# A graph transformer layer with a mixture of experts: index loads first, the lane chain ahead of the last four tiles, and a final stage with 21 buffers

## The reference

```
xn = layernorm(x)
x1 = x + l2norm([xn, mean of xn[src] over dst] @ W) + bias + linear_attention(xn)
x2 = layernorm(x1)
# router: graph attention over the 131072 edges and one loop per node, 4 heads, 4 experts
e     = leaky_relu(a_src[src] + a_dst[dst])          # a = x2 @ (W_gat . att)
alpha = softmax of e over the edges of one dst
agg   = sum of h[src] * alpha over dst               # h = x2 @ W_gat
score = mean over heads of layernorm(agg + b)
gate  = softmax of the two best scores, 0 elsewhere
out = x1 + sum over the 4 experts of gate[e] * (gelu(x2 @ W1[e] + b1[e]) @ W2[e] + b2[e])
```

## Time and profile before

| | |
|---|---|
| Time, median of 3 runs | 5569.49 us (5564.70 to 5574.14) |
| The profiled execution | 5532.89 us, its span 5531.1 us |
| PE busy | 3498.8 us, 63% of the span |
| POOL busy | 2828.8 us, 51% |
| DVE busy | 2089.8 us, 38% |
| ACT busy | 793.1 us, 14% |
| HBM | 392.03 MB read, 146.74 MB written |

### The profile page before, as it was taken

The page is one execution under the profiler, slowest core; times in us unless marked ns, Lnnn a source line. Parts: engine busy times, 40 slices in busy tenths (PEclk is TensorE's granted clock), DMA queues, the critical chain, the costliest instruction groups (busy, mean ns, idle before and its releaser), DMA issues.

```text
span 5531.1 us, 46201 instructions
## 1 busy us (share of the span) xinstructions
PE 3498.8 (63%) x12938; PEld 2286.8 (41%) x12938; DVE 2089.8 (38%) x4906; ACT 793.1 (14%) x1914; POOL 2828.8 (51%) x2951
## 2 busy tenths in 40 slices
PE   0688888888577777777242766666666666669300
PEld 0455555555455545555121443434343434346200
DVE  5466665566466545444110111202021111103288
ACT  4111111111011111111010101111111111112000
POOL 2666666666666666666657044445445353530420
PEclk6799999899788889888575888787778878789755
DMA  7444444444355555555121011111111111111287
GB/s 241 127 116 114 114 114 114 111 115 113 109 137 147 149 143 157 167 150 147 23 57 19 32 49 33 47 35 44 38 43 46 36 46 36 46 31 63 85 258 258
DMA packets 381412, 540.56 MB, mean 98 GB/s; under 512 B 120314, under 2 KB 297818, under 8 KB 381143
## 3 DMA queue, kind: packets, MB, share of 16 engines
q0 software_dynamic: 119136, 234.44, 17.7%
q1 hardware_dynamic: 239503, 284.45, 15.8%
q10 hardware_dynamic: 22632, 20.15, 1.1%
HBM read 392.03 MB, written 146.74 MB: 97 GB/s over the span
## 4 chain that ended last, share of the span: by engine, by line
PE 24%; another core or an unknown queue 13%; issue 7%; DVE 3%; DVEq 2%; DMA 1%; ACT 0%; SPq 0%; ACTq 0%
PE PS L1668 14%; PE PS L1660 10%; DVE acc L1589 2%; DVEq L1588 1%; DMA out<-acc 1%; ACT hid L1629 0%; DMA x2g<-x_turned 0%; DVE rec L1418 0%; DVE y_sb L1603 0%; DVE sc L1553 0%; SPq L1287 0%; DVE rden L1528 0%; ACTq L1649 0%; DVE q L1523 0%
## 5 line engine op out<-in xcount | busy, mean ns | idle before, releaser
L773 POOL DMA_INDIRECT rows<-xn_rows,gsrc x1664 | 1606.2, 965 | 881.2 <-issue 455.9
L1339 POOL DMA_INDIRECT nb<-route_rows,idx x1024 | 999.6, 976 | 1082.8 <-DVE msg L1414 767.7
L1668 PE MATMUL PS<-arena,hid 128*125 128x256 f32 x3200 | 771.0, 400 | 555.6 <-ACT hid L1629 339.4
L1078 PE MATMUL PS<-rows,oh 128*128 128x257 f32 x3328 | 891.2, 421 | 281.5 <-issue 207.2
L1660 PE MATMUL PS<-x2g,arena 128*128 128x500 f32 x1600 | 754.6, 631 | 284.8 <-issue 148.3
L1668 PEld LDWEIGHTS PS<-arena,hid 128*125 128x125 f32 x3200 | 632.8, 199 | 710.7 <-issue 578.9
L1603 DVE TENSOR_TENSOR y_sb<-PS,b_b 125x512 f32<-125x512 f32 x200 | 128.7, 685 | 2004.6 <-PE PS L1668 1467.7
L1078 PEld LDWEIGHTS PS<-rows,oh 128*128 128x128 f32 x3328 | 684.9, 212 | 411.3 <-issue 242.9
L1660 PEld LDWEIGHTS PS<-x2g,arena 128*128 128x128 f32 x1600 | 319.6, 203 | 698.7 <-issue 535.7
L1629 ACT ACTIVATE hid<-PS,b_sb 128x500 f32<-128x500 f32 x400 | 270.3, 677 | 1547.5 <-PE PS L1660 758.5
L1150 PE MATMUL PS<-own_w,p_t 128*125 128x512 f32 x400 | 237.2, 678 | 124.4 <-issue 68.8
(11 more groups left out here) (303 smaller groups left out, 3093.0 us busy)
## 6 DMA issues: line engine op xcount, KB each, us to landing
y_rows<-y_sb SPq DMA_DIRECT2D x100, 512.0 KB
arena<-y_rows SPq DMA_DIRECT2D x100, 512.0 KB
rows<-xn_rows,gsrc POOLq DMA_INDIRECT x1664
nb<-route_rows,idx POOLq DMA_INDIRECT x1024
sum_rows<-kept SPq DMA_DIRECT2D x104, 128.5 KB
x_rows<-x SPq DMA_DIRECT2D x100, 128.0 KB
hid<-x_rows SPq DMA_DIRECT2D x100, 128.0 KB
m_in<-sum_rows SPq DMA_DIRECT2D x100, 125.5 KB
```

The source lines that it names most:

```text
L773: pool.indirect_dma_start(out=rows[w][h][:, q, 0:D], out_offset=None, in_=xn_rows, in_offset=bass.IndirectOffsetOnAxis(ap=gsrc[:, s * HU + ...
L1078: last = mm(SUM[:, 0:D + 1], oh[w][h][:, q, :], rows[w][h][:, q, :], start=h == 0 and q == 0, stop=h == 1 and q == HU - 1)
L1339: pool.indirect_dma_start(out=nb[b % NBUF][:, c, :], out_offset=None, in_=route_rows, in_offset=bass.IndirectOffsetOnAxis(ap=idx[:, b * W ...
L1668: last = mm(Y[j % 2][e // 2][0:NP, (e % 2) * D:(e % 2 + 1) * D], hid[:, 4 * e + k, j * NP:(j + 1) * NP], w2_sb[:, e, k, :], start=k == 0, ...
```

## The change

Parameters and the order of DVE's and SP's work change in all three parts.

In the first block SP loads the graph's indices first and then batches 2 and 3 of x; ACT loads only 0 and 1. ACT sums 0, 2, 4, 5 and 6, DVE's statistics stay for 1 and 3, POOL scales 3 and 4.

```diff
-LN_BY_DVE = (1, 3, 5)
-LN_BY_POOL = (0, 2, 4)
+LN_BY_DVE = (1, 3)
+LN_BY_POOL = (3, 4)
+LN_ROOTS = (0, 2, 1, 4, 3, 5, 6)
+LN_SCALED = (0, 2, 1, 5, 6)
@@ SP, after the stores of the chunks' limits
+                store_x(0, s_xs[0])
+                store_x(2, s_xs[2])
+                load_x(4, s_xs[0])
+                store_x(1, s_xs[1])
+                load_x(6, s_xs[2])
+                load_x(5, s_xs[1])
+                for b in (3, 4, 5, 6):
+                    store_x(b, s_xs[3])
@@ ACT
-                for b in range(LN_RING):
+                for b in range(2):
                     for of, to in ln_rows(x, b):
                         act.dma_start(to, of).then_inc(s_xa[b], 16)
```

```diff
                 walk(dve, POST_AT + NT + 7, [
-                    
+                    (0, 0, SORTED_AT, sort_low),
...
-                    (POST_AT + 3, 0, NT, second_norm), (2, 0, NT, spread),
+                    (POST_AT + 3, 0, NT, second_norm), (2, 0, NT, spread), (0, 0, SORTED_AT, sort_high),
...
-                    (0, 0, SORTED_AT, sort_low), (0, 0, SORTED_AT, sort_high), (0, 0, SORTED_AT, sort_turn)], plain=SORTED_AT)
+                    (-1, 1, NS, one_hot), (POST_AT, 0, NT, mean), (0, 0, SORTED_AT, sort_turn)], plain=SORTED_AT)
```

```diff
-    t = int((b + 1) * 5.65) + 3
-    return t if t % 4 < 2 else t + 4 - t % 4
+    t = int((b + 1) * 6.06 + 5.5)
+    t = t if t % 4 < 2 else t + 4 - t % 4
+    return NT if b == NB - 1 else min(t, LANES_AT - 3)
@@ DVE
+                    if t == LANES_AT - 1:
+                        for b in late:
+                            scores(b)
+                            records(b)
+                        lane_ends()
+                        over_lanes()
+                        lane_sums()
+                        first_maxima()
+                        first_records()
+                    if t == NT - 3:
+                        weigh(0)
@@ ACT
+                    if 4 * g == LANES_AT:
+                        for b in late:
+                            act.wait_ge(s_dif, b + 1)
+                            a(dd[:], dd[:], ACT.Exp).then_inc(s_ex, 1)
```

```diff
-YR = 8
-AR = 4
-FT = 20
+YR = SPARE + 16
+AR = 10
+FT = 10
@@ DVE
+                    if t % 2 == 0:
+                        dve.wait_ge(s_cmb, t // 2 + 1)
+                        v.tensor_tensor(acc[t % AR], CMB[t // 2 % CB][0:NP, 0:D], x1_in[q][0:NP, :], ALU.add).then_inc(s_acc, 1)
+                        return
...
                 for k in range(FG):
-                    weigh(k)
+                    if k + 1 < FG:
+                        weigh(k + 1)
                     for t in range(k * FT, (k + 1) * FT):
-                        combine(t)
+                        add_rows(t)
@@ ACT, in each group behind the exponential of the scores
+                        if t == k * FT:
+                            act.wait_ge(s_gt, k + 1)
+                            if k + 2 < FG:
+                                load_own(act, k + 2)
+                        if t % 2 == 0:
+                            if t // 2 >= DG:
+                                act.wait_ge(s_cmb, t // 2 - DG + 1)
+                            for e in range(NE):
+                                last = a(diag[t // 2 % DG][:, e, :], ident[0:NP, 0:NP], ACT.Copy, scale=gate[:, t, e:e + 1])
+                            last.then_inc(s_diag, 1)
+                        if t >= FT:
+                            store_out(t - FT)
@@ PE, behind the last group
+                pe.wait_ge(s_yc, NT)
+                for t in range(0, NT, 2):
+                    pe.wait_ge(loaded(t), in_group(t))
+                    pe.wait_ge(s_diag, t // 2 + 1)
+                    if t // 2 >= CB:
+                        pe.wait_ge(s_acc, t - 2 * CB + 1)
+                    for e in range(NE):
+                        last = mm(CMB[t // 2 % CB][0:NP, 0:D], diag[t // 2 % DG][:, e, :], y_in[t % YR][0:NP, e * D:(e + 1) * D], start=e == 0, stop=e == NE - 1)
+                    last.then_inc(s_cmb, 1)
```

More of the change, by code:

```diff
@@ L45 @@
 NBUF = 3
-YR = 8
-AR = 4
-FT = 20
+SPARE = 5
+YR = SPARE + 16
+AR = 10
+FT = 10
+DG = 3
+CB = 8
+YG = 3
 FG = NT // FT
-AHEAD = 4
+AHEAD = 8
+ADS_EARLY = 40
 EVEN = 112
@@ L283, in build @@
         s_xd = sem("s_xd")
-        s_xs = [sem(f"s_xs{u}") for u in range(2)]
+        s_xs = [sem(f"s_xs{u}") for u in range(4)]
         with nc.Block() as block:
@@ L317, in _, with store_x @@
                 sp.dma_start(hi_b, to_all(chunk_hi.rearrange("c o -> o c"))).then_inc(s_crb, 16)
-                for b in range(LN_BATCHES):
+                def store_x(b, done):
                     if b in LN_BY_POOL:
@@ L362, in _ @@
                 act.wait_ge(s_v, 2)
-                for b in range(LN_BATCHES):
+                for b in LN_ROOTS:
                     if b in LN_BY_DVE:
@@ L775, in _ @@
                                                 ).then_inc(s_rows[w][(h * HU + q) // QUAD], 16)
-                for t in range(NT):
+                for t in range(ADS_EARLY):
                     pool.wait_ge(s_hc, t + 2)
@@ L1267, in build, with store_records, load_own @@
             s_ys = [ev(f"s_ys{u}") for u in range(2)]
-            s_yl = [ev(f"s_yl{q}") for q in range(YR)]
+            s_yl = [ev(f"s_yl{q}") for q in range(YR // YG)]
+            loaded = lambda t: s_yl[t % YR // YG]
+            in_group = lambda t: 32 * sum(i % YR // YG == t % YR // YG for i in range(min(NT, (t // YR + 1) * YR)))
             s_acc = ev("s_acc")
-            s_out = [ev(f"s_out{q}") for q in range(AR)]
-            batches_after = lambda t: [b for b in range(NB) if unit_after(b) == t]
-            LAST = unit_after(NB - 1)
-            assert LAST + 4 < NT and LAST // 4 == NG - 2
+            s_gt = ev("s_gt")
+            s_diag = ev("s_diag")
+            s_cmb = ev("s_cmb")
+            s_out = [ev(f"s_out{q}") for q in range(AR // 2)]
+            stored = lambda t: s_out[t % AR // 2]
+            batches_after = lambda t: [b for b in range(NB) if unit_after(b) == t]
+            late = batches_after(NT)
+            assert len(late) == 1
+            def store_records(eng, b):
+                eng.wait_ge(s_rec, b + 1)
+                eng.dma_start(rec_rows[0:EF, :].rearrange("(p f) c -> p f c", p=P)[:, b * W:(b + 1) * W, :],
+                             rec[b % 2][:]).then_inc(s_recs[b % 2], 16)
+            def load_own(eng, k):
+                if k:
+                    eng.wait_ge(s_own, 16 * k)
+                if k >= 2:
+                    eng.wait_ge(s_gt, k - 1)
+                eng.dma_start(own[k % 2][:], route_rows[k * FT * NP:(k + 1) * FT * NP, :].rearrange("(t p) c -> p t c", p=NP)).then_inc(s_own, 16)
             @block.sync
@@ L1322, in _ @@
-                for q in range(AR):
-                    sp.wait_ge(s_out[q], 32 * NT // AR)
+                    if t == AT_AD:
+                        sp.wait_ge(s_ends, 1)
+                    if t == AT_PE:
+                        load_own(sp, 1)
+                    load_x1(t)
+                    if t >= AT_PE:
+                        load_y(t)
+                for t in range(YR, NT):
+                    sp.wait_ge(s_acc, t - YR + 1)
+                    load_x1(t)
+                    load_y(t)
@@ L1325, in _ @@
+                for q in range(AR // 2):
+                    sp.wait_ge(s_out[q], 64 * NT // AR)
             @block.gpsimd
@@ L1330, in _ @@
                                         pattern=[[1, 4], [-1, 4]], channel_multiplier=0).then_inc(s_fe, 1)
+                for t in range(ADS_EARLY, NT):
+                    pool.indirect_dma_start(out=ad_rows, out_offset=bass.IndirectOffsetOnAxis(ap=start_i[:, t:t + 1], axis=0),
+                                            in_=ad_all[:, t, :], in_offset=None).then_inc(s_ads, 16)
                 pool.indirect_dma_start(out=ad_first[:], out_offset=None, in_=route_rows,
@@ L1646, in _ @@
                     for t in range(k * FT, (k + 1) * FT):
-                        act.wait_ge(s_acc, t + 1)
-                        for lo, hi in ((0, EVEN), (EVEN, NP)):
-                            act.dma_start(out[t * NP + lo:t * NP + hi, :], acc[t % AR][lo:hi, :]).then_inc(s_out[t % AR], 16)
+                        if t == k * FT:
[10 more added lines that the diff above has]
+                            store_out(t - FT)
+                for t in range(NT - FT, NT):
+                    store_out(t)
             @block.tensor
@@ L1653, in _, with turn_ends @@
                 mm = nc.tensor.matmul
+                def turn_ends():
+                    pe.wait_ge(s_ends, 1)
+                    for k in range(4):
+                        last = nc.tensor.transpose(HP[0][0:20, k * P:(k + 1) * P], ends[:, k, :], ident)
+                    last.then_inc(s_endt, 1)
+                    pe.wait_ge(s_ends, 2)
+                    nc.tensor.transpose(HP[1][:, 0:20], fm[:, 0:P], ident[0:20, 0:20])
```

(1 more changed line is left out.)

156 lines of the change are left out of this document (75 added, 81 removed).

## The result

The changed kernel takes 5609.39 us (median of 6 runs, 5602.74 to 5633.02), the kernel before 5569.40 in 6 runs beside it: a ratio of 1.0077 (95% interval 1.0063 to 1.0091). It is slower by 43 us by the ratio, where 64 less was forecast. The profiled execution of the changed kernel took 5609.28, its span is 5607.4.

A forecast was written before the change was run, and what follows sets the result against it. Unbroken runs of POOL's indirect DMAs were taken to let other engines start only one instruction at a time. Terms: -21 + 0 - 50 + 68 + 0 - 61 = -64, so 5505 us for the median; 8-in-10 range 5440 to 5565.

The forecast's parts named there:

- Drains between the scans: Expert stage, DVE: some 2.5 us for each of 16 batches, taken as nothing (0 to 16 us more).
- My own reading, that a run costs nothing until it has gone on for a while: POOL's unbroken indirect DMAs first cost other engines nothing, then let them start one instruction at a time.
- Final stage and last tiles: From the copy of tile 92 to the end: +388 instead of +449, so 61 us less (30 to 80).
- crawl: Other engines start one instruction at a time during POOL's long indirect-DMA runs; PE does a matmul per 2.18 us.
- steady groups: Final stage: groups of ten tiles, weighs 28.3 us apart (26 to 31).
- third rival: Final stage hangs on ACT: own's load delays what follows, a group takes 36 us, no gain there; 5566, chance 0.13.
- Scatters split: 40 scatters stay at the graph block's end, 50 us less (40 to 60); 60 precede expert gathers, 68 more (50 to 80).
- first rival: Run length is no lever, slow stretches belong to their places; both terms of the split vanish: 5487, chance 0.10.
- First block: Loads and sums of x redistributed over engines: ends at 112 instead of 133, 21 us less (10 to 27).
- AHEAD of 8: Start of the expert stage: two pauses of about 3 us vanish from POOL's run, crawl starts some 10 us earlier.
- fourth rival: Slower: gathers' backlog makes the graph block's crawl, nothing gained there; expert start still pays 68: 5592, chance 0.12.

The follow-up runs named there:

- c0: The changed kernel itself, run and profiled again on a later occasion: 5599.05 us, 1.0071 times the kernel before.
- e9: The changed kernel itself, run again in the third set: 5541.32 us, 1.0024 times the kernel before.
- before again: The kernel before, unchanged, profiled a second time: span 5559.4 us; its median on that occasion was 5564.8 us.
- c1: The changed kernel without the drains between the 20 scans, in one set with c0: 5531.38 us, 0.9945 times the kernel before.
- e1: The changed kernel with AHEAD 4 instead of 8: 5612.10 us, 1.0075 times the kernel before.
- e3: The changed kernel without the drains between the 20 scans, first set: 5533.22 us, 0.9936 times the kernel before.
- e10: The changed kernel without scan drains, with own loaded on SP and all scatters in the graph block: 5460.66 us, 0.9883 times the kernel before.
- e6: The changed kernel with every own loaded on SP, own(1) ahead of the last tiles' stores: 5502.32 us, 0.9949 times the kernel before.
- e7: The changed kernel with all 100 scatters in the graph block again: 5540.80 us, 1.0010 times the kernel before.
- c3: e10 with a drain on POOL before every 8th gather of the router: 4823.06 us, 0.8665 times the kernel before.
- d1: e10 with a drain on POOL before every 12th router gather and every 8th scatter: 4698.49 us, 0.8497 times the kernel before.
- c2: The changed kernel, drains kept, with one POOL drain ahead of each batch's fourth gather: 5550.71 us, 0.9977 times the kernel before.
- d2: e10 with POOL drains before every 16th router gather, every 8th scatter and every second set of graph row gathers: 5096.34 us, 0.9234 times the kernel before.
- e2: The changed kernel with AHEAD 2 instead of 8: 5314.53 us, 0.956 times the kernel before.
- e8: The kernel before with AHEAD 2, without the rest of the change: 5229.42 us, 0.9434 times the kernel before.

## Why the prediction was wrong

Forecast -64, measured +43 (+37 in c0's set, +13 in e9's). By its steps, from "before again" to c0:

- **Drains between the scans: "I take nothing (0 to 16 more)".** This step failed. I asked whether DVE had the 2.5 us per batch, and it has (3.6 us as measured, 0.19 per drain). What I did not ask is who runs beside the scans: POOL, whose run is held by them without drains and not with them. They cost 68 (c0 and c1) to 79 us (e1 and e3); of the 68, 59 lie between the first group and tile 92, over 13 runs, and 9 behind it. On the occasion of e9 and e10 they cost some 39. My own reading, that a run costs nothing until it has gone on for a while the earlier trace rows, gave the means: what takes a pause out of a run costs time. I used it for the scatters and not for the scans.
- **Final stage and last tiles: -61, measured about -22** (-55 in the final stage, +33 on the way from tile 92 to the last tile; in the profile of after 119 us against the +113 I had). The gaps of 19.68 and 5.46 are near the 16 to 18 and 7 predicted, and the steady groups are right. I had excluded a crawl in runs of 20 gathers; the one shown above lies beside such a run. gate(1) came at 5337.81, +150 against +134, after a wait for own(1) on SP's queue that I had not counted, and the second group took 47.5. That group is the third rival's mechanism, in single groups instead of all: load of own on ACT, with stores queued behind it. e6 prices both at 39 us; without them the term would have been right.
- **Scatters split: -50 and +68.** The direction and the near cancellation were right, the first size was not: by e6 and e7 it is -75, outside the 40 to 60 given, and +76 (in the table -77 with the first block, and +79). The first group was to take 340 us; it takes 360. The first rival, that run length is no lever, is out: by c3 and d1 it is the largest lever of this kernel. What the prediction drew for it from the Trainium skill ("Runtime: NRT & Kernel Launch", Instruction fetch mechanics), that PE is not slowed by what POOL issues, does not agree with these runs; whether fetching has a part in the slowing no run shows.
- **First block: -21, measured -6** (132.9 to 127.2), outside the bounds of 10 to 27. The sums end 10.5 us earlier instead of some 20, because batch 4 came at 66.3 and not at 58, and POOL's scaling of batch 3 took 1.38 us per instruction on average. That is the form that subtracts `ln_mv`; the form with `nm` right behind it takes 0.56, as before. I had taken POOL's scaling as free. Why it is slow was not tried.
- **AHEAD of 8.** I gave it 10 us of earlier crawl; e1 shows no difference.

Without the drains, own's places and the split, e10 is at 0.9883, 65 us less than before. By the forecast's own terms such a kernel stood at -82 (the first block's 21 and the 61). The last tiles and the final stage bear theirs out, with some 70 less in e10's profile; the first block does not. That 65 is so near the 64 of the whole forecast is chance.

The fourth rival's side (slower) came true, by another mechanism than the one that I gave it: the graph block did gain, and more than forecast.

## What to carry to other kernels

An instruction that looks free on its own engine is to be priced also by what its slowness or its speed does to the engine beside it: here drains on DVE kept POOL from being held, and POOL's longer unbroken run slowed PE and ACT. Where a profile shows the other engines starting few instructions while POOL issues indirect DMAs without a break, try a drain every dozen, and search the number by runs: 8, 12 and 16 gathers gave middles of 1664, 1579 and 1826 us here. A load of small rows on a queue of stores can hold up what stands behind it, here for 17 us; put it where nothing waits behind it.

## What the runs showed of the hardware that was not expected

- Indirect DMAs issued by POOL at a pitch of 1.25 to 1.35 us slow the other engines; on ACT it first showed 13 to 17 us after the last pause (c0, c1, c2). Pauses of 2.5 us after 8 gathers (c3) and of 2.7 after 12 (d1) leave the first group at some 70 us; 2.8 after 16 (d2) do not. What in the chip is short is not shown by any run.
- 20 scans on DVE back to back make one gather on POOL beside them take 3.3 to 4.4 us instead of 1.06, in all 13 runs of c1 and of the kernel before; with drains between them they do not.
- Four or eight gathers ahead make no difference (e1); two make the kernel 4 to 6% faster (e2, e8), without ending the crawl (e8).
- The same kernel before ran at 5528 to 5569 us on different occasions, and the changed kernel stood to it at 1.0024 to 1.0077.
